# The edge stage of a graph network: messages in three bf16 parts instead of float32, one buffer per slot, and loop bounds stored as two values

## The reference, cut to what matters

```python
def _L3_gnn_ref(h, edge_index, edge_attr, msg_w1, msg_b1, msg_w2, msg_b2, upd_w1, upd_b1, upd_w2, upd_b2):
    src, dst = (edge_index[0], edge_index[1])
    m_in = jnp.concatenate([h[src], h[dst], edge_attr], axis=1)
    msg = jax.nn.relu(m_in @ msg_w1 + msg_b1) @ msg_w2 + msg_b2
    agg = jax.ops.segment_sum(msg, dst, num_segments=h.shape[0])
    upd_in = jnp.concatenate([h, agg], axis=1)
    upd = jax.nn.relu(upd_in @ upd_w1 + upd_b1) @ upd_w2 + upd_b2
    return h + upd
```

## Time and profile before

| what | value |
|---|---|
| median of three runs | 4103.77 us |
| span of the profiled execution | 4131.5 us |
| mean granted TensorE clock | 0.913 |
| PE busy | 3483.2 us, 84% of the span, 23502 instructions |
| PE weight loads busy | 2445.5 us, 59% |
| DVE busy | 1463.3 us, 35%, 4278 instructions |
| ACT busy | 1265.5 us, 31%, 4012 instructions |
| POOL busy | 871.1 us, 21%, 928 instructions |

### The profile page before, as it was taken

The page is one execution under the profiler, slowest core; times in us unless marked ns, Lnnn a source line. Parts: engine busy times, 40 slices in busy tenths (PEclk is TensorE's granted clock), DMA queues, the critical chain, the costliest instruction groups (busy, mean ns, idle before and its releaser), DMA issues. The chain is left out here.

```text
span 4131.5 us, 85615 instructions
## 1 busy us (share of the span) xinstructions
PE 3483.2 (84%) x23502; PEld 2445.5 (59%) x23503; DVE 1463.3 (35%) x4278; ACT 1265.5 (31%) x4012; POOL 871.1 (21%) x928
## 2 busy tenths in 40 slices
PE   5888889999988888968999999997777677776777
PEld 2345556777744434435999999985444445444545
DVE  6766667777601200024431111132222222222223
ACT  5566667878701300014322211232000000000001
POOL 2000000000010000000000000024666566666663
PEclk8999999999999999997999999997777778787778
DMA  2011222333495589861432222341222222222222
GB/s 60 1 46 62 69 70 87 106 101 119 133 231 127 136 188 230 196 169 31 124 107 78 76 77 77 89 115 48 65 63 63 60 63 63 62 63 63 61 63 55
DMA packets 120056, 381.79 MB, mean 92 GB/s; under 512 B 33166, under 2 KB 74620, under 8 KB 106026
## 3 DMA queue, kind: packets, MB, share of 16 engines
q1 hardware_dynamic: 90958, 324.81, 29.5%
q0 software_dynamic: 25664, 51.90, 5.7%
q10 hardware_dynamic: 3154, 1.60, 0.2%
HBM read 294.59 MB, written 83.62 MB: 92 GB/s over the span
## 5 line engine op out<-in xcount | busy, mean ns | idle before, releaser
L2266 POOL DMA_INDIRECT edge_rows<-src_table,src_idx x784 | 776.6, 991 | 471.2 <-issue 193.4
L685 ACT ACTIVATE build_scaled<-build_lanes,w 128x128 f32<-128x128 bf16 x1132 | 428.6, 405 | 307.4 <-DVE build_lanes L640 275.0
L756 PE MATMUL build_ps<-build_keys,build_scaled 128*128 128x300 bf16 (+1 forms) x2264 | 492.2, 299 | 20.5 <-ACT build_scaled L685 17.8
L640 DVE TENSOR_SCALAR build_lanes<-key_id,lane,one_w 128x128 f32<-128x128 f16 x1132 | 389.1, 344 | 237.9 <-PE build_ps L756 181.9
L2410 ACT ACTIVATE edge_act<-edge_ps 128x512 f32<-128x512 f32 x196 | 116.9, 597 | 1147.6 <-remote 741.7
L2382 PEld LDWEIGHTS edge_ps<-edge_hot,edge_act 128*128 128x128 f32 x1760 | 297.8, 244 | 263.5 <-issue 261.5
L1108 PE MATMUL prop_ps<-prop_rows,y 125*128 125x500 f32 (+1 forms) x1050 | 408.3, 546 | 50.0 <-DMA prop_rows<-adj_rows 43.2
L2360 PE MATMUL edge_ps<-m_store,edge_hot_t 125*128 x2640 | 269.1, 249 | 205.0 <-issue 126.0
L748 PE MATMUL build_ps<-build_keys,build_lanes 128*128 128x300 bf16 (+1 forms) x1132 | 345.3, 305 | 87.8 <-DVE build_keys L642 65.4
L642 DVE TENSOR_SCALAR build_keys<-key_id,key,win_base 128x300 bf16<-128x300 f16 (+1 forms) x1132 | 406.0, 359 | 0.5 <-issue 0.2
L2382 PE MATMUL edge_ps<-edge_hot,edge_act 128*128 x1760 | 316.3, 332 | 94.8 <-issue 58.9
(11 more groups left out here) (368 smaller groups left out, 4762.4 us busy)
## 6 DMA issues: line engine op xcount, KB each, us to landing
prop_rows<-adj_rows SPq DMA_DIRECT2D x85, 1367.2 KB
cnt_panels<-build_cnt SPq DMA_DIRECT2D x50, 683.6 KB
adj_rows<-build_adj_t SPq DMA_DIRECT2D x25, 1367.2 KB
n<-cnt_panels SPq DMA_DIRECT2D x40, 683.6 KB
orders_panel<-cnt_panels SPq DMA_DIRECT2D x40, 683.6 KB
edge_dst_row<-dst_rows SPq DMA_DIRECT2D x196, 125.0 KB
h<-cnt_panels SPq DMA_DIRECT2D x20, 683.6 KB
prop_rows<-adj_rows SPq DMA_DIRECT2D x85, 158.7 KB
```

The costliest lines, as they stand in the source:

```text
L640: v.tensor_scalar(lanes[s][:], g.key_id[:, 0:128], g.lane[:, at], g.one_w3[:, at], ALU.is_equal, ALU.mult).then_inc(s_lanes[s], 1)
L685: a.activation(scaled[s][:], half(lanes[s], 1), ACT.Copy, scale=g.w12[:, bass.ds(t, 1)]).then_inc(s_scaled[s], 1)
L756: last = pe.matmul(ps[:, weight_bank(j), 0:KW[j % 2]], half(scaled[s], i), keys[s][:, 0:KW[j % 2]], start=False, stop=False, skip_group_ch ...
L2266: pool.indirect_dma_start(rows[s][:, i, :], None, dr.table, bass.IndirectOffsetOnAxis(ap=g.src_idx[:, t:t + 1], axis=0)).then_inc(s_rows[s ...
```

## The change

It does four things in the edge stage, and one small thing before it.

1. **The relu'd messages become three bf16 parts.** ACT writes relu(x) as bf16 into `act[s][:, 0]`. DVE forms max(x, 0) minus that part into a float32 tile `left`; ACT rounds `left` to bf16 as part 1; DVE subtracts again for part 2. The sums are then 12 bf16 matmuls a block (4 tiles by 3 parts) where there were four float32 ones.
2. **Buffers by slot.** `hot_t`, and the semaphores that say it is full or free, exist once per slot and no longer alternate by a running count. `hot` and the PSUM bank of the sums exist once. The waits in DVE's code are now:

The diff, cut to its core:

```diff
-        self.eng.reg_mov(self.now[0], both >> RANGE_BITS)
-        self.eng.reg_mov(self.now[1], both & (RANGE - 1))
-        lo = self.eng.snap(self.now[0], min_val=0, max_val=NB - 1)
-        end = self.eng.snap(self.now[1], min_val=1, max_val=NB)
+        of = self.nxt if ahead else self.now
+        lo = self.eng.snap(of[0][s], min_val=0, max_val=NB - 1)
+        end = self.eng.snap(of[1][s], min_val=1, max_val=NB)
...
-        act = [ph.sb(f"act{s}", [128, GT, D]) for s in range(SLOTS)]
-        hot = ph.sb("hot", [128, 2, GT * B])
-        hot_t = ph.sb("hot_t", [B, 2, W], BF16)
+        act = [ph.sb(f"act{s}", [128, 3, W], BF16) for s in range(SLOTS)]
+        left = [ph.sb(f"left{i}", [128, W]) for i in range(2)]
+        hot = ph.sb("hot", [128, GT * B], BF16)
+        hot_t = [ph.sb(f"hot_t{s}", [B, W], BF16) for s in range(SLOTS)]
...
+            def parted(r, s):
+
+                v.wait_ge(s_high[s], r + 1)
+                v.scalar_tensor_tensor(left[s % 2][:], ps[:, s, :], 0.0, act[s][:, 0, :], ALU.max,
+                                       ALU.subtract).then_inc(s_left[s], 1)
+                v.wait_ge(s_mid[s], r + 1)
+                v.tensor_tensor(act[s][:, 2, :], left[s % 2][:], act[s][:, 1, :], ALU.subtract).then_inc(s_low[s], 1)
 
             def round_of(r, last):
                 for s in range(SLOTS):
-                    if s + 2 < SLOTS:
-                        turned(r, s + 2, False)
+                    sums(r, s)
+                    if s + 3 < SLOTS:
+                        turned(r, s + 3, False)
                     elif not last:
-                        turned(r + 1, s + 2 - SLOTS, True)
-                    sums(r, s)
+                        turned(r + 1, s + 3 - SLOTS, True)
+                    if s + 1 < SLOTS:
+                        parted(r, s + 1)
+                    elif not last:
+                        parted(r + 1, 0)
...
             def sums(r, s):
-                pe.wait_ge(s_act[s], r + 2)
+                pe.wait_ge(s_low[s], r + 1)
...
-                    pe.wait_ge(s_hot, n)
-
-                    pe.wait_ge(s_added, n)
+                    pe.wait_ge(s_hot, summed.next())
                     for i in range(GT):
-                        last = pe.matmul(bank, act[s][:, i, :],
-                                         hot[:, bass.ds(here, 1), i * B:(i + 1) * B].rearrange("p a k -> p (a k)"),
-                                         start=i == 0, stop=i == GT - 1)
+                        for p in range(3):
+                            last = pe.matmul(ps[:, SUMS, 0:B], act[s][:, p, i * 128:(i + 1) * 128],
+                                             hot[:, i * B:(i + 1) * B], start=i == 0 and p == 0,
+                                             stop=i == GT - 1 and p == 2)
...
-                    a.activation(act[s][:].rearrange("p a k -> p (a k)"), ps[:, s, :], ACT.Relu).then_inc(s_act[s], 1)
+                    a.activation(act[s][:, 0, :], ps[:, s, :], ACT.Relu).then_inc(s_high[s], 1)
+                    a.wait_ge(s_left[s], a.snap(r + 2))
+                    a.activation(act[s][:, 1, :], left[s % 2][:], ACT.Copy).then_inc(s_mid[s], 1)
```

More of the change, by code:

```diff
@@ L2187, in __init__ @@
         self.eng, self.g = eng, g
-        self.cur = [eng.alloc_register(name=f"group{i}") for i in range(SLOTS)]
-        self.nxt = [eng.alloc_register(name=f"group_next{i}") for i in range(SLOTS)]
-        self.now = [eng.alloc_register(name=f"group_now{k}") for k in range(2)]
-        eng.load(self.cur, g.groups[0:1, 0:SLOTS])
-        eng.load(self.nxt, g.groups[0:1, SLOTS:2 * SLOTS])
+        self.now, self.nxt = ([[eng.alloc_register(name=f"group_{turn}{k}{i}") for i in range(SLOTS)] for k in range(2)]
+                              for turn in ("now", "next"))
+        for k in range(2):
+            eng.load(self.now[k], g.groups[0:1, k, 0:SLOTS])
+            eng.load(self.nxt[k], g.groups[0:1, k, SLOTS:2 * SLOTS])
     def advance(self, r):
-        for c, n in zip(self.cur, self.nxt):
-            self.eng.reg_mov(c, n)
-        self.eng.load(self.nxt, self.g.groups[0:1, bass.ds(r * SLOTS + 2 * SLOTS, SLOTS)])
+        for k in range(2):
+            for now, nxt in zip(self.now[k], self.nxt[k]):
+                self.eng.reg_mov(now, nxt)
+            self.eng.load(self.nxt[k], self.g.groups[0:1, k, bass.ds(r * SLOTS + 2 * SLOTS, SLOTS)])
     def each(self, s, ahead, body):
-        both = self.eng.snap((self.nxt if ahead else self.cur)[s], min_val=0, max_val=NT * RANGE)
-        self.eng.reg_mov(self.now[0], both >> RANGE_BITS)
-        self.eng.reg_mov(self.now[1], both & (RANGE - 1))
-        lo = self.eng.snap(self.now[0], min_val=0, max_val=NB - 1)
-        end = self.eng.snap(self.now[1], min_val=1, max_val=NB)
+        of = self.nxt if ahead else self.now
+        lo = self.eng.snap(of[0][s], min_val=0, max_val=NB - 1)
+        end = self.eng.snap(of[1][s], min_val=1, max_val=NB)
         with self.eng.Fori(lo, end) as d:
@@ L2229, in edge_phase @@
         s_ea = [ph.sem(f"ea{s}") for s in range(SLOTS)]
-        s_hot_t = ph.sem("hot_t")
-        s_free = ph.sem("free")
+        s_hot_t = [ph.sem(f"hot_t{s}") for s in range(SLOTS)]
+        s_free = [ph.sem(f"free{s}") for s in range(SLOTS)]
         s_pre = [ph.sem(f"pre{s}") for s in range(SLOTS)]
-        s_act = [ph.sem(f"act{s}") for s in range(SLOTS)]
+        s_high = [ph.sem(f"high{s}") for s in range(SLOTS)]
+        s_left = [ph.sem(f"left{s}") for s in range(SLOTS)]
+        s_mid = [ph.sem(f"mid{s}") for s in range(SLOTS)]
+        s_low = [ph.sem(f"low{s}") for s in range(SLOTS)]
         s_hot = ph.sem("hot")
         s_sum = ph.sem("sum")
-        s_added = ph.sem("added")
         s_tick = ph.sem("tick")
@@ L2272, in _ @@
             blocks = Blocks(v, g)
-            made = Counter(v)
+            made = [Counter(v) for s in range(SLOTS)]
             added = Counter(v)
@@ L2293, in one @@
                 def one(d):
[L2294 to L2298 removed]
+                    v.wait_ge(s_free[s], made[s].next())
+                    v.tensor_scalar(hot_t[s][:], dst_row[s][:], g.block_base[0:B, bass.ds(d, 1)], lane[0:B, :],
+                                    ALU.add, ALU.is_equal).then_inc(s_hot_t[s], 1)
                 blocks.each(s, ahead, one)
@@ L2354, in one @@
                 def one(d):
-                    n = used.next()
-                    here = pe.snap(n & 1, min_val=0, max_val=1)
-                    pe.wait_ge(s_hot_t, n)
+                    pe.wait_ge(s_hot_t[s], used[s].next())
                     for i in range(GT):
                         for p in range(3):
-                            last = pe.matmul(ps[:, s, i * 128:(i + 1) * 128], hot_t[:, bass.ds(here, 1), i * 128:(i + 1) * 128]
-                                             .rearrange("p a k -> p (a k)"),
+                            last = pe.matmul(ps[:, s, i * 128:(i + 1) * 128], hot_t[s][:, i * 128:(i + 1) * 128],
                                              a3.q_parts[:, bass.ds(d, 1), p, :].rearrange("p a k -> p (a k)"),
                                              start=False, stop=False, skip_group_check=True)
-                    last.then_inc(s_free, 1)
+                    last.then_inc(s_free[s], 1)
                 blocks.each(s, ahead, one)
```

46 lines of the change are left out of this document (17 added, 29 removed).

## The result

The changed kernel takes 4131.09 us (median of five runs, 4118.21 to 4145.08) against 4099.78 us for the kernel before (five runs, 4084.48 to 4116.94). The ratio is 1.0089, with a 95% interval of 1.0061 to 1.0117: 31 us slower, by the interval 25 to 48. In a later set of runs it was 1.0115 (1.0088 to 1.0143), 48 us. It is within about 1% in the one and just outside in the other, always on the slow side. The profiled execution after has a span of 4128.5 us, 2.6 us under its median. The one before lay 27.7 us above its own, so the two spans hide the difference, and I compare them by stretches.

A forecast was written before the change was run, and what follows sets the result against it. The prediction took PE's semaphore updates, held during POOL's gather bursts, to bound the edge stage. All terms were 0 except +61 us for single buffers, so 4104 + 61 = 4165 us; forecast range 4120 to 4230, 8 in 10 from 4020 to 4270.

The forecast's parts named there:

- The mechanism with the chance of 0.40: Edge stage: POOL's bursts hold PE's updates, and single buffers add held exchanges in two-block groups; +61 us, chance 0.40.
- What bounds the kernel: Edge stage: PE's semaphore updates are held during POOL's burst, let go about 0.9 us after; 6.0 us a group.
- the first rival: Edge stage: PE is the bound and the change is faster, 3940 us, or partly so 4050; chance 0.25.
- The sums on PE: PE's sum matmuls in bf16: 47 us less work, hidden behind the hold; value 0, bounds -47 and 0.
- Register instructions: Fewer a slot, PE 28 to 13, DVE 23 to 13; hidden behind the hold; value 0, bounds -114 and 0.
- DVE and ACT: Two more DVE operations a group, 247 us more busy, and one ACT copy; fits into 6.3 us; value 0.
- Longer gathers: POOL's gathers starting during DVE operations with two SBUF inputs take longer; value 0, bounds -37 and +37.
- The single buffers: One `hot_t` a slot, one `hot`: held exchanges in 24 two-block groups; +61 us, bounds 0 and +180.
- The signs: If right: relus 0.8 to 1.0 us after bursts, POOL 6.3 us a group or more, PE busy about 50 us less.
- PE was the bound: Edge stage: PE sets the pace, so the change is faster, 3940 us, or partly so 4050; chance 0.25.
- Groups of two blocks cost nothing: The hold stays, but updates slip through between gathers: 4104 us, or 4110 with a little left; chance 0.24.
- The chain through one `hot` bounds every group: Sum, update, addition, `hot`, next sum strictly in turn; 0.8 us a group lost, 157 us, 4261 us; chance 0.11.

The follow-up runs named there:

- b_sum1: Kernel before with one float32 sum matmul a block instead of four: 4063.24 us against 4095.49, ratio 0.992.
- b_gather3: Kernel before with three gathers a group instead of four from the second round on: 3847.66 us, ratio 0.9385.
- b_one: Kernel before with every group's range cut to its first block, in the faster set: 3861.09 us, ratio 1.0002.
- a_both2: Changed kernel with two `hot_t` per slot, `hot` and the sums' bank double, `hot` ahead of the addition: 4106.11 us, ratio 0.9991 to the kernel before.
- a_one: Changed kernel with every group's range cut to its first block, in the faster set: 3881.60 us, ratio 1.0053 to the kernel before.
- b_hot1: Kernel before with a single `hot` and a single sums' bank, DVE's addition ahead of `hot`: 4104.16 us against 4095.49, ratio 1.0015.
- a_one_again: Changed kernel with every group's range cut to its first block, with held updates: 4069.25 us against 4106.18 for the kernel before, ratio 0.9893.
- b_pair: Kernel before with POOL waiting for two slots' updates, so that it makes two bursts and pauses once: 4211.23 us, ratio 1.0287.

## Why the prediction was right, and where it was off

I had forecast 4165 us, a loss of 61, and 31 to 48 came. The mechanism with the chance of 0.40 is the one at work: held updates and single buffers, in the groups of two blocks. That the size came so near is partly luck, as the term of the single buffers shows below.

- **What bounds the kernel.** Right. 237 us less work on PE gave 32 us (b_sum1), 1.24 us less burst gave its whole worth (b_gather3), and in the timeline of the changed kernel the sums' update comes 4.5 us late while PE stands idle. My picture of the hold, let go some 0.9 us after a burst, was too strict: that update came between the sixth and seventh gather of eight, the one for `hot_t` 1.8 us after the last gather. The rule by which I let the first rival live, that an update can trail a matmul's recorded end because the engine has not finished (the Trainium skill, Perfetto Trace Analysis, "Tensor Engine Instruction"), does not account for that: the same kinds of matmuls in b_one had their updates within 0.05 us.
- **The sums on PE, value 0.** Right for the time. Their busy time fell by 70 us where I had said 47: the 2640 matmuls of L2383 are 245.9 us busy, and not the 269.1 of L2360 by which I priced them. By the rate of b_sum1 (32 of 237) 70 us are worth some 9 us.
- **Register instructions, value 0.** Not measured. a_both2 cannot price them, since its double buffers bring most of them back. The traces show more than I had read from them: in the kernel before, 182 register instructions of PE and 83 of DVE that wait for nothing take over 0.5 us each, 0.7 us as a rule, 181 us in sum; in the changed kernel there are none. What that is worth in time stays open. It may hide a part of what the single buffers cost.
- **DVE and ACT, value 0.** Right: 217 us more busy on DVE (I had said 247; the two operations sum to 270, and a part of that overlaps other work of DVE) and nothing in the time of a_both2.
- **Longer gathers, value 0, bounds -37 and +37.** Here the sum became smaller by 17 us, not larger (759.9 against 776.6), with updates held. Between b_one and a_one, in the faster set, it was +16 us, and there it counted in full.
- **The single buffers, +61.** The term that decided, and right in kind: a_both2 prices it at 51 us, net of the register instructions. Its parts were sized wrong in both directions. I had 2.7 us for an exchange of `hot_t` and 2.5 for one of `hot`; the two timelines have POOL waiting 5.82 and 4.82. Against that, not every exchange is held: of DVE's 24 waits for `s_free` PE's matmul ended 8 promptly, a third, near the 31% that I took from POOL's waits. And b_hot1 shows that the single `hot` with its new order costs the kernel before 9 us in all. The two would agree if the usual group gains from the order what the 24 groups lose: the relus' median interval fell from 6.26 to 6.09 us in b_hot1 and to 6.01 in the changed kernel. That is read from traces and not isolated, and how the 51 us split between `hot` and `hot_t` stays open. The 25 us that I allowed for the cost of such groups before fit the trace of before (195 intervals, mean 0.13 us above the median), but the run that was to test them, b_one, fell into the set where they cost nothing.
- **The signs.** POOL needs 6.42 us a group (2830.4 to 4088.1), PE's busy time fell by 76 us and its idle time grew, and DVE waits 6.37 us for a sum, "remote", after a first block: as forecast. The relus do not all start 0.8 to 1.0 us after a burst's last gather: one timeline has 1.14 us (2942.77 after 2941.63), and 61 of the 196 start while a gather runs, where 28 did before.
- **PE was the bound (0.25).** Refuted by b_sum1 and b_gather3.
- **Groups of two blocks cost nothing (0.24).** Refuted for the changed kernel by a_one_again: without their second blocks it is 80 to 91 us faster.
- **The chain through one `hot` bounds every group (0.11).** Refuted: without second blocks the changed kernel, with its one `hot`, is 1.1%, 44 us (37 by the medians), faster than the whole kernel before, more than the 25 us estimated for disturbances before, and at a granted clock of only 0.69 in the stage. My sign for it, a clock well below 0.78, did appear (0.73) and did not mean it.

The step that the prediction lacked altogether is the condition on all this. It took the hold as given for every execution; in the faster set there was none. Its own sign for "PE was the bound", a relu that follows its matmul in the midst of a burst, appeared there, and POOL was the bound and not PE.

No version that does the whole work beats the kernel before: a_both2 is level with it.

## What to carry to other kernels

Before pricing work saved on an engine, look in the timeline at how late its semaphore updates arrive, and at whose activity they arrive late: if they do, the number of exchanges per period counts for most, and a second buffer can be worth more (51 us here) than faster operations (32 us for 237 us of work). Price a single buffer by the cases that pass through it twice in a period, however few: 24 groups of 196 made the difference here. And packing an engine's work together to save a pause can cost more than the pause: in b_pair it cost 116 us.

## What the runs showed of the hardware

- **Updates of PE's semaphores are held behind POOL's gathers in some sets of runs and not in others.** Three sets and the first measurement had before at medians of 4095 to 4109 us, one had it at 3862 (3851 to 3874). With the hold, updates came 4.5 and 6.5 us after the matmuls' end; without it all 196 relus of b_one started within 0.05 us of it. All kernels of a set were alike in this. That POOL's gathers are what holds them is read from the timelines and from b_gather3; gathers alone do not do it, since b_one has them back to back. The faster set and a later one with held updates carry the same chip number, so the chip alone does not explain it; what switches it stays open. The busy stages ahead of the edge stage are no different (2565 us of PE work in the first 2830 us before, 2562 in b_one).
- **Register instructions were slow in the same sets.** 182 of PE and 83 of DVE took over 0.5 us in the stage of the kernel before, none in b_one, and none in the changed kernel, which has half as many. The cause stays open.
- **A gather that begins shortly after a DVE operation with two SBUF inputs takes up to 1.46 us instead of 0.944.** With one SBUF input the longest took 1.085 us.
- **A faster stage can have a higher granted clock, or a lower one.** With one gather fewer the stage's clock rose from 0.78 to 0.87 and the same 5576 matmuls took 798 us and not 898; with three quarters of the sums removed the stage was faster too, and the clock fell to 0.70.
